# Filler products before score pairs that follow the rows' work, and in eight narrow half steps

## The reference, cut to what matters

```python
h = layernorm(x) * (1 + ca) + sa
q, k, v = per-head 16x16 products of h        # scale 256 ** -0.25 on q and k
scores  = where(j > i, -inf, q @ k.T)         # 4096 x 4096 for each of 16 heads
y       = softmax(scores) @ v
x       = x + ga * (y @ Wu.T + bu)
h       = layernorm(x) * (1 + cb) + sb
x       = x + gb * ffn(h)                     # 16 experts, 4 chosen of 2 groups, and a shared one
```

## Time and profile before

| | us |
|---|---|
| median of 3 runs | 2142.78 |
| lowest, highest | 2141.27, 2144.37 |
| the profiled execution, its own time | 2135.55 |
| its span | 2133.8 |
| PE busy | 2036.8 (95%) |
| DVE busy | 1684.6 (79%) |
| ACT busy | 1405.7 (66%) |
| POOL busy | 647.3 (30%) |
| mean granted clock of PE | 0.987 of full |

### The profile page before, as it was taken

One profiled execution on the slowest core, in us unless ns is written; L12 is line 12 of the kernel. 1 busy time (PEld: TensorE's weight loads), 2 busy tenths in 40 slices (PEclk: granted clock), 3 DMA queues, 4 the chain that ended last, 5 costly groups with the idle time before them and its releaser, 6 DMA issues. The chain is left out here.

```text
span 2133.8 us, 44373 instructions
## 1 busy us (share of the span) xinstructions
PE 2036.8 (95%) x17927; PEld 1090.0 (51%) x17927; DVE 1684.6 (79%) x2173; ACT 1405.7 (66%) x2742; POOL 647.3 (30%) x867
## 2 busy tenths in 40 slices
PE   7999999999999999999999999999999898999996
PEld 5543333444444444344444433444444787888886
DVE  7788888999999878899999988777777764555554
ACT  5356677788888878678888888677766333444442
POOL 2011111110111111111111120303346573878777
PEclk9999999999999999999999999999999899999998
DMA  6542311123411211431211131000012644555552
GB/s 217 156 76 58 63 38 36 44 70 62 94 47 47 63 47 43 84 76 37 70 49 50 64 116 58 18 17 21 21 37 69 260 163 129 123 118 121 115 121 46
DMA packets 123695, 167.72 MB, mean 79 GB/s; under 512 B 17457, under 2 KB 95794, under 8 KB 122722
## 3 DMA queue, kind: packets, MB, share of 16 engines
q1 hardware_dynamic: 109328, 147.40, 24.4%
q0 software_dynamic: 14016, 17.45, 4.6%
q10 hardware_dynamic: 146, 0.03, 0.0%
HBM read 89.96 MB, written 76.03 MB: 78 GB/s over the span
## 5 line engine op out<-in xcount | busy, mean ns | idle before, releaser
L1023 DVE TENSOR_REDUCE mx<-S 128x2 f32<-128x1024 f32 (+3 forms) x1152 | 1277.6, 1134 | 162.3 <-PE S L890 114.1
L993 ACT ACTIVATE prob<-ST 128x512 f32<-128x512 f32 (+3 forms) x2304 | 1168.1, 559 | 333.3 <-PE ST L911 251.8
L937 PE MATMUL O<-prob,V 128*17 128x256 f32 (+1 forms) x8704 | 670.5, 380 | 1.0 <-POOL prob L858 1.0
L890 PE MATMUL S<-K,Q 48*128 48x512 f32 (+3 forms) x2304 | 552.6, 476 | 22.2 <-DVE mx L1023 19.4
L911 PE MATMUL ST<-Q,K 49*128 49x512 f32 (+3 forms) x2304 | 477.8, 411 | 27.8 <-ACT prob L993 22.7
L890 PEld LDWEIGHTS S<-K,Q 48*128 48x128 f32 x2304 | 215.1, 183 | 443.3 <-issue 280.3
L858 POOL TENSOR_SCALAR_AFFINE_SELECT prob<-prob 128x512 f32<-128x512 f32 x128 | 81.8, 639 | 873.1 <-ACT prob L993 873.1
L937 PEld LDWEIGHTS O<-prob,V 128*17 128x17 f32 x8704 | 144.6, 95 | 289.9 <-issue 279.3
L911 PEld LDWEIGHTS ST<-Q,K 49*128 49x128 f32 x2304 | 217.6, 185 | 111.3 <-ACT prob L993 89.5
L1765 PE MATMUL gate_up<-hhi,wup 128*128 128x512 f32 x608 | 204.6, 397 | 0.0
L1888 ACT ACTIVATE sg<-gate_up 128x512 f32<-128x512 f32 x92 | 55.1, 599 | 161.5 <-PE gate_up L1765 161.4
(11 more groups left out here) (244 smaller groups left out, 1626.5 us busy)
## 6 DMA issues: line engine op xcount, KB each, us to landing
late<-cwt SPq DMA_DIRECT2D x76, 256.0 KB, 3.9
lists<-wbd SPq DMA_DIRECT2D x132, 138.0 KB, 2.3
parts<-wcut SPq DMA_DIRECT2D x108, 128.0 KB, 2.1
units<-parts SPq DMA_DIRECT2D x18, 768.0 KB, 12.4
Q<-qs SPq DMA_DIRECT2D x192, 64.0 KB, 2.4
xs<-lists SPq DMA_DIRECT2D x19, 552.0 KB, 3.8
K<-ks SPq DMA_DIRECT2D x18, 512.0 KB, 9.3
wraw<-in_wcat SPq DMA_DIRECT2D x54, 128.0 KB, 2.2
```

The costliest lines, as they stand in the source:

```text
L890: ins = pe.matmul(out[:, ab, 0:w], Q[g, n % QR, p, r * P:(r + 1) * P], K[G % 2][g, p, c * BW:c * BW + w], start=True, stop=not diag)
L937: ins = pe.matmul(O[32 * a:32 * a + VC, c0:c1], V[:, G, k, VC * a:VC * (a + 1)], prob[:, s % NP, a, c0:c1], start=s in FIRST and h == 0, s ...
L993: act.activation(prob[:, s % NP, 2 * p + ab, c0:BW], ST[i % ST_BANKS][:, c0:BW], ACT.Exp).then_inc(s_exp, 1)
L1023: dve.tensor_reduce(mx[:, n % 2, a:a + step + 1:step, c], S[slot % S_RING][:, :, 0:w], AX_X, ALU.max).then_inc(s_free, 1)
```

## The change

Two edits, both in `attention_order`.

```diff
@@ in scores(now, most)
-            fillers = 2 if sent[0] < 6 else 4 if now < FIRST[1] else (3 if again else 1) if now < FIRST[2] else 2 if again and now < FIRST[NB] else 0
+            fillers = 2 if sent[0] < 6 else 4 if now < FIRST[1] else (3 if again else 1) if now < FIRST[2] else 3 if ringed[0] else 2 if again and now < FIRST[NB] else 0
@@ in the loop over the steps
         events.append(("ST", (s, 1)))
+        if k > TPB * j + 1 and G in (1, 2) and j < 2:
+            fill(2)
         if s in LAST:
             ask(LAST.index(s) + 1)
```

## The result

The changed kernel took 2163.66 us in the median of 4 executions (2157.5 to 2176.24), the kernel before 2143.57 (2141.27 to 2144.39, 4 executions): a ratio of 1.0084, 95% interval 1.0053 to 1.0115. It is slower by 20 us. Run again in more executions beside before, it was slower by 8 us: 2145.15 against 2136.93 (ratio 1.0038, 1.0025 to 1.0050) and, on another chip, 2145.62 against 2137.92 (1.0037, 1.0016 to 1.0057). The 8 us are the price of the fillers; what the first result has beyond them has another cause.

The account below looks back on a forecast made before the run. TensorE, busy 95% of the span, was taken to bound the kernel, with little slack beside VectorE. Terms 5.8 + 2.0 - 3.1 - 0.6 = +4.1 us on the 2142.78 median gave 2146.9 us, range 2137 to 2152.

Parts of the forecast that it names:

- the two drops of the earlier trace: Half-clock stretches in attention at 899.16 to 905.99 and 1568.18 to 1578.42 us, costing 3.0 and 4.5 us.
- the count of places: 28 score pairs in the last head group get 84 fillers; 8 half steps about one group change get 16.
- the price of a filler: Three fillers before a score pair cost 0.33 us straight behind rows' work, 0.43 behind an O item.
- The first edit, 5.8 us: Fillers at the last head group's 28 places add 6.4 us, less 0.6 given back by waits.
- The second edit, 2.0: Fillers at 8 half steps about the group change add 2.6 us, less 0.6 hidden in waits for VectorE.
- The filler's own wait: Each filler's wait for the exponential three turns back costs nothing; 2.8 us if it bound everywhere for 0.1 us.
- The clock, 3.7 us back: Fillers keeping the clock up in attention return 3.1 us at the long drop and 0.6 at the group change.
- 7 in 10: Chance that fillers after the count of places, in a 1.00 us gap, prevent the long drop: 3.1 of 4.5 us.
- The 44%: Share of a half-clock stretch in attention lost: an item took 2.48 us against 1.40.
- Rival A: Fillers in TensorE's gaps before score pairs and about the group change save the clock: -6.6 us, 2136.2; chance 0.28.
- B: Fillers on the path at every logit half and copy, no drop saved: +12.5 us, 2155.3; chance 0.14.
- C: Fillers and clock cancel at some 3 us each, or neither clock nor end moves: 2142.8 us; chance 0.14.

Follow-up runs that it names:

- e1: The changed kernel without the two fillers at the group change, leaving three fillers at 28 places of the last head group; 2146.39 us, ratio 1.0015 to before.
- e3: Only the last head group's three-filler edit, and only before step 552 (blocks j = 6 to 3); 2142.54 us, ratio 1.0016 to before.
- e7: Only the last head group's three-filler edit, and only from step 552 (blocks j = 2 and 1); 2139.23 us, ratio 1.0018 to before.
- e6: Only the last head group's edit, with six fillers instead of three at each of the 28 places; 2150.96 us, ratio 1.0068 to before.
- e2: Only the second edit, 16 fillers about the change from the second to the third head group; 2138.57 us, ratio 0.9999 to before.
- e4: Only the last head group's edit, without its filler products, keeping the wait for ScalarE ahead of them; 2141.62 us, ratio 1.0006 to before.
- e11: The second edit alone, run once more: 16 fillers about the change from the second to the third head group; 2143.48 us, ratio 1.0010 to before.
- e9: The second edit, plus fillers in the last head group's narrow half steps of block j = 1 and waits of block j = 0; 2138.40 us, ratio 1.0005 to before.
- e5: The changed kernel run again without any edit, in more executions; 2145.15 us, ratio 1.0038 to before.
- e10: The changed kernel run a third time without any edit, on a third chip; 2145.62 us, ratio 1.0037 to before.
- e8: The second edit, plus three fillers after the count of places and after the turning of y for query block 3; 2143.87 us, ratio 1.0035 to before.

## Why the prediction was wrong

It forecast +4.1 us, 2146.9 in a range of 2137 to 2152, and gave slower 0.38. The result, 2163.66, lies outside, 16.8 us above the forecast. The later medians, 2145.15 and 2145.62, lie inside, but against before on the same chips they are +8.2 and +7.7 us, twice the forecast.

*One reading of the earlier trace rows was wrong.* The slice at 8 isn't inside attention. It runs from 1653.7 to 1707.1 us, and attention ends at 1654.6. Of some 59 us at half clock in that trace only 17 lie in attention, the two drops of the earlier trace rows.

*What bounds the kernel, the count of places, the price of a filler: right.* The places after a half of the logits (a PL item at 1462.30, three fillers, the score pair) and after a projection, in the trace after:

```profile
1434.41 3.72 PE L1263 MATMUL S<-row_space 128*128 128x256 f32 x16
1437.97 0.49 PE L919 MATMUL ST<-maskh,idh 128*128 128x256 bf16 x3
1438.39 0.51 PE L892 MATMUL S<-K,Q 48*128 48x512 f32 x2
...
1439.62 0.51 PE L892 MATMUL S<-K,Q 48*128 48x512 f32 x2
...
1462.30 1.06 PE L1272 MATMUL S<-row_space 128*128 128x16 f32 x8
1463.21 0.49 PE L919 MATMUL ST<-maskh,idh 128*128 128x256 bf16 x3
1463.63 0.51 PE L892 MATMUL S<-K,Q 48*128 48x512 f32 x2
```

The same two in the trace before:

```profile
1432.99 3.72 PE L1261 MATMUL S<-row_space 128*128 128x256 f32 x16
1436.64 0.50 PE L890 MATMUL S<-K,Q 48*128 48x512 f32 x2
...
1460.29 1.07 PE L1270 MATMUL S<-row_space 128*128 128x16 f32 x8
1461.29 0.50 PE L890 MATMUL S<-K,Q 48*128 48x512 f32 x2
```

From the logits to the score pair 1.33 us instead of 1.00, and from the projection 3.98 instead of 3.65: 0.33 in both. Behind an O item the other price holds: from the O products to the score pair 0.99 us with three fillers (1460.08 to 1461.07), 0.55 without (1438.70 to 1439.25 before), so 0.44 where 0.43 was taken. After the projection the next score pair follows 1.23 us later, not 1.39 as before (1436.64 to 1438.03) and as in the earlier trace rows. VectorE's copy seems to be done by then: 0.16 is hidden, where 0.17 was forecast.

*The first edit, 5.8 us: right in kind, a little low.* At full clock the blocks 6 to 1 are 1.4, 1.2, 1.3, 0, 1.0 and 1.5 us longer, 6.4 in all, which is the sum before I took two small waits off it. By the line of executions it is 8.0 (e1), or 5.4 + 2.0 (e3, e7); of the 1.6 us between 6.4 and 8.0 about 1 is within what the line can tell, and no trace shows the rest. The block of CN and of the 1 us waits costs nothing even with six fillers (e6): there VectorE, busy 46 of 52 us, sets the pace (PE waits 5.7 us for it in e2's trace of that block).

*The second edit, 2.0: high.* Some 1.5 us by blocks, 1.0 by the line.

*The filler's own wait, nothing: right* (e4).

*The clock, 3.7 us back: this is the step that failed.* The prediction said: "The CN fillers fall into the gap of 1.00 us that precedes the long drop [...] I give them 7 in 10 to keep the clock up: 0.7 x 4.5 = 3.1 us." The drop did go, but it was worth 1.3 us, not 4.5: block j = 3 took 53.4 us with it and 52.1 without. The 44% were read off two items that PE bounds and laid on a block that VectorE bounds. Where PE does bound, they hold: 3.0 us for the drop at the group change (23.0 against 20.0), and 7.3 of 17.1 us in e3's block j = 1. Longer drops in block j = 3 cost more: 4.2 us for 17.1 (e11) and 5.4 for 20.5 (e9). Over all executions a microsecond at half clock costs 0.36.

Behind that is a larger fault. I took the two drops of one trace for properties of two places and priced their removal. The 13 traces show half clock in attention at changing places, and the 90 executions of before spread over more than 30 us along its line. Behind attention the places don't change, whatever the kernel: in all 13 a stretch of 10.2 us begins 27 to 31 us after attention's end, and 13 to 15 us stand at the very end of the program, which the fillers can't reach. In the median the changed kernel has as much half clock as before (55.7 against 55.5 us on e5's chip and 55.7 against 55.6 on e10's). In the mean there are 3.3 and 4.8 us less, worth 1.2 and 1.7 us. So the return was 0 to 2 us, and 7.8 of fixed cost less that gives +6 to +8, where the repeats gave +8.2 and +7.7.

The chance of 7 in 10 isn't refuted. Block j = 3 kept full clock in five of the seven traces with fillers after CN (not in e1 and e10), and in one of the six without (e2); its mean length was 52.5 against 54.2 us. Thirteen traces don't settle whether the fillers did that, and no run had the CN fillers alone. Even if they did, it is 1.7 us and not 3.1. Rival A took the 7.2 us between the timed and the profiled runs of before for half clock. The spread along the line fits that, but no kernel with fillers returned nearly the 7.5 to 10.5 us that rival A needed.

*The 20 us of the first four executions.* Their recorded half clock is 89.8 us in the mean, 25 to 31 more than before has in the table, worth 9 to 11 us: the clock, forecast to give 3.7 us back and at worst to take 3.0, took about 10. Another 7 us stand above the line of the same program in e5 and e10, in each of the four. With the 8 of the fillers that makes some 25 us over a usual before of 2137 to 2139; the before run beside them had 2143.57, so 20 are left.

The trace that I have of them shows PE late behind its records from some 1600 us on, as above, which would be half clock that wasn't recorded. Part of the 7 us can be placed: block j = 2 is 4.9 us longer than in e5 with 6.8 us recorded, which at 0.44 explain 3.0. And from attention's end to the last gate and up product it took 465.3 us, against 458.2 to 461.0 in the other twelve traces, with 30 us recorded there against 20 to 27. That is an argument from one trace, not shown. Why those four drew so much, whether the chip or the moment, stays open: two more chips didn't repeat it.

*The rivals.* B (+12.5) came nearest to the first result and overshot the repeated one; its "filler on the path" at every place is refuted by the 0.16 that hides and by block 3. C is refuted by the repeats, whose intervals begin at 1.0025 and 1.0016.

## What to carry to other kernels

Filler work on the busiest engine has a sure price, which the rows of one trace gave here as 7.8 us against 8.0 to 8.2 measured; what it buys is a chance. Before pricing a clock drop away, see whether it stands at the same place in a second trace, and how many microseconds of time a microsecond at half clock costs in that block, which is little where another engine sets the pace. And where the time depends on the clock, compare kernels at equal clock (time against mean clock, over all executions), since four executions can differ from twelve by more than the change does.

## What the runs showed of the hardware

With full clock, blocks of attention of 57 to 80 us repeat within 0.1 us over three chips, so nearly all the spread of this program, from 2132 to over 2160 us, is the granted clock. Stretches at half clock were 3.4 to 37.5 us long. In attention their place and length moved from execution to execution: at the group change 6.8, none or 37.5 us in kernels that don't differ there, though the same few starts came back (857 to 859 us in four traces, 887 to 888 in four others). In the expert part they stood at the same place after attention's end in all 13 traces. With fillers in its waits the last block kept full clock in e9's one trace, as it did in six others without them; and e8 shows that a gap filled in one place is no promise of less half clock in all.
